# Another split of the scan steps over the engines, and the gate product moved by half a tile

## The reference

```python
def step(h, inp):
    u_t, dt_t, B_t, C_t = inp
    dA = jnp.exp(jnp.clip(dt_t[..., None] * A, -20.0, 0.0))
    dB_u = jnp.clip(dt_t[..., None] * B_t[:, None, :] * u_t[..., None], -10.0, 10.0)
    h = jnp.clip(h * dA + dB_u, -100.0, 100.0)
    y = jnp.einsum('bds,bs->bd', h, C_t)
    return (h, y)
...
y = y * jax.nn.silu(z)
```

## Time and profile before

| | |
|---|---|
| Time, median of 3 runs | 5121.12 us (5117.18 to 5122.27) |
| The profiled execution, its own time | 5121.12 us |
| Its span on the core | 5119.3 us |
| POOL line 2237 (X), 512 instructions | 1190.1 us busy, 2362 ns each |
| POOL line 2244 (Z), 128 instructions | 302.1 us busy, 2360 ns each |
| DVE line 2422 (Z), 256 instructions | 313.5 us busy, 1225 ns each |
| The last copy of `yp` | starts at 4159.86 us |

### The profile page before, as it was taken

The page is one execution under the profiler, slowest core; times in us unless marked ns, Lnnn a source line. Parts: engine busy times, 40 slices in busy tenths (PEclk is TensorE's granted clock), DMA queues, the critical chain, the costliest instruction groups (busy, mean ns, idle before and its releaser), DMA issues. The chain is left out here.

```text
span 5119.3 us, 48377 instructions
## 1 busy us (share of the span) xinstructions
PE 4267.1 (83%) x15605; PEld 2378.9 (46%) x15605; DVE 3493.2 (68%) x3850; ACT 2150.4 (42%) x3741; POOL 2645.8 (52%) x1523
## 2 busy tenths in 40 slices
PE   8997977699999099888748888888888869978886
PEld 6776865344444044333224444444444434435553
DVE  5554347422476456378869999999999967745776
ACT  1111114222354711067736655656655643423442
POOL 4445964000132011057859999999999953312221
PEclk9998986699999599899869999999999989989998
DMA  3422232323487845334451151151151135530000
GB/s 106 117 83 63 80 107 99 133 93 107 158 297 258 342 181 197 133 133 169 171 198 57 59 182 58 57 182 61 55 184 62 51 116 189 197 109 9 34 33 33
DMA packets 364678, 634.08 MB, mean 124 GB/s; under 512 B 67494, under 2 KB 153287, under 8 KB 352274
## 3 DMA queue, kind: packets, MB, share of 16 engines
q1 hardware_dynamic: 327378, 588.07, 32.9%
q10 hardware_dynamic: 37056, 43.00, 2.3%
HBM read 402.83 MB, written 228.15 MB: 123 GB/s over the span
## 5 line engine op out<-in xcount | busy, mean ns | idle before, releaser
L2237 POOL TENSOR_TENSOR sc_X<-sc_Bm,sc_w 128x1024 f32<-128x1024 f32 x512 | 1190.1, 2362 | 25.2 <-DMA sc_Bm<-d_xd 24.9
L2364 PE MATMUL sc_yp<-sc_Z,sc_idn 128*128 128x512 f32 x1536 | 724.6, 605 | 79.7 <-DVE sc_Z L2422 76.7
L2259 ACT ACTIVATE sc_A<-sc_dt,keep_A 128x1024 f32<-128x1024 f32 x512 | 574.7, 1123 | 288.0 <-DVE sc_Z L2422 222.8
L1329 PE MATMUL ff_ps<-ffn_R 128*128 128x512 f32 x1536 | 660.6, 593 | 0.7 <-issue 0.7
L2364 PEld LDWEIGHTS sc_yp<-sc_Z,sc_idn 128*128 128x128 f32 x1536 | 278.2, 192 | 421.7 <-issue 269.7
L1329 PEld LDWEIGHTS ff_ps<-ffn_R 128*128 128x128 f32 x1536 | 291.7, 190 | 364.1 <-issue 363.6
L2351 PE MATMUL sc_yp<-sc_idn,sc_hT 128*128 128x128 f32 x2048 | 262.7, 282 | 131.1 <-ACT sc_hT L2292 131.1
L2244 POOL TENSOR_TENSOR sc_Z<-sc_H,sc_Cm 128x1024 f32<-128x1024 f32 x128 | 302.1, 2360 | 63.1 <-DVE sc_H L2417 63.0
L2351 PEld LDWEIGHTS sc_yp<-sc_idn,sc_hT 128*128 128x128 f32 x2048 | 238.2, 192 | 199.3 <-ACT sc_hT L2292 199.3
L2422 DVE TENSOR_TENSOR sc_Z<-sc_A,sc_Cm 128x1024 f32<-128x1024 f32 x256 | 313.5, 1225 | 8.8
L2292 ACT ACTIVATE sc_hT<-sc_tp,sc_ct 128x128 f32<-128x128 f32 x1024 | 288.8, 366 | 52.2 <-PE sc_tp L2344 52.1
(11 more groups left out here) (380 smaller groups left out, 8124.5 us busy)
## 6 DMA issues: line engine op xcount, KB each, us to landing
sc_Bm<-d_xd SPq DMA_DIRECT2D x64, 512.0 KB, 7.1
ffn_gate_d<-ff_o SPq DMA_DIRECT2D x96, 256.0 KB, 2.2
ffn_up_d<-ff_o SPq DMA_DIRECT2D x96, 256.0 KB, 6.2
ffn_g_d<-ff_z SPq DMA_DIRECT2D x24, 1024.0 KB, 6.5
ffn_R<-ffn_g_d SPq DMA_DIRECT2D x8, 3072.0 KB, 10.9
ffn_R<-ffn_up_d SPq DMA_DIRECT2D x8, 3072.0 KB, 21.3
sc_Cm<-d_xd SPq DMA_DIRECT2D x48, 512.0 KB, 7.5
ffn_R<-ffn_up_d SPq DMA_DIRECT2D x23, 1024.0 KB, 12.9
```

Source lines behind the costliest of these rows:

```text
L1329: last = nc.tensor.matmul(ps[:, 2 + t % 6], w[:, k, h * P:(h + 1) * P], xt[:, n, k], start=(k == 0), stop=(k == KD - 1))
L2237: nc.gpsimd.tensor_tensor(X[:, k % RX], Bm[:, n], w[:, j % 2], ALU.mult).then_inc(db, 1)
L2259: nc.scalar.activation(A[:, k % 2], dt[:, j % 2], ACT.Exp, scale=keepA[:, n:n + 1]).then_inc(ex, 1)
L2364: last = nc.tensor.matmul(yp[:, e * TB:(e + 1) * TB], idn[:], Z[:, zed(k) % RZ, e * TB:(e + 1) * TB], start=(n == 0), stop=(n == NS - 1))
```

## The change

- `ON_POOL` goes from states 3, 6, 9, 12 to 3, 6, 10, 13, and `ON_PE` from 1, 4, 7, 10 to 1, 4, 8, 12. So DVE multiplies for states 0, 2, 5, 7, 9, 11, 14, 15, and no longer for 0, 2, 5, 8, 11, 13, 14, 15. The counts stay 4, 4 and 8.
- PE's gate products move from the first four steps of each 8 to the last four. With that `keep_z` of tile t moves from step 4 of tile t to step 1 of tile t + 1, and the z store from step 7 of tile t to step 3 of tile t + 1. The last `keep_z` and the last z store come after the loops.
- The first loads of the gate's operands come one state later in SP's list.

```diff
--- before.py
+++ after.py
@@ -2050,8 +2050,8 @@
 TC = 1024
 
 
-ON_POOL = (3, 6, 9, 12)
-ON_PE = (1, 4, 7, 10)
+ON_POOL = (3, 6, 10, 13)
+ON_PE = (1, 4, 8, 12)
 
 
 def scan_stage(nc, keepA, flag, ident, win_t, dt_d, w_d, xd_d, xt_d, y_d, z_d):
@@ -2191,9 +2191,9 @@
             load_rows(0)
             for n in range(NS):
                 load_b_c(0, n)
-                if n < KD:
-                    load_xz(0, n)
-                    load_wz(0, n)
+                if 1 <= n <= KD:
+                    load_xz(0, n - 1)
+                    load_wz(0, n - 1)
             load_dt_w(1)
             for k in range(NU_):
                 i, c, n = place(k)
@@ -2220,9 +2220,11 @@
                     load_wz(t + 1, q)
                     if (t + 1) % CB == 0:
                         load_xz(t + 1, q)
-                if k % UZ == UZ - 1:
-                    sp.wait_ge(zev, 1 + t + 1)
-                    sp.dma_start(z_d[t % CB * P:(t % CB + 1) * P, t // CB * TB:(t // CB + 1) * TB], zo[:]).then_inc(zst, 16)
+                if k % UZ == 3 and t:
+                    sp.wait_ge(zev, 1 + t)
+                    sp.dma_start(z_d[(t - 1) % CB * P:((t - 1) % CB + 1) * P, (t - 1) // CB * TB:((t - 1) // CB + 1) * TB], zo[:]).then_inc(zst, 16)
+            sp.wait_ge(zev, 1 + NT)
+            sp.dma_start(z_d[(CB - 1) * P:CB * P, (T // TB - 1) * TB:T], zo[:]).then_inc(zst, 16)
             sp.wait_ge(zst, 1 + NT * 16)
 
         @block.gpsimd
@@ -2314,14 +2316,15 @@
                     decay(k + 2)
                 if n == NS - 1:
                     store(k // NS)
-                if k % UZ == KD:
-                    keep_z(k // UZ)
+                if k >= UZ and k % UZ == 1:
+                    keep_z(k // UZ - 1)
                 if on_pe(n - 1):
                     turn(k - 1, 0)
                 if on_pe(n - 2):
                     turn(k - 2, 1)
                 if n == 0 and c == CB - 1 and i + 1 < NCH:
                     columns(i + 1)
+            keep_z(NT - 1)
             act.wait_ge(yst, 1 + NU_ // NS * 16)
 
         @block.tensor
@@ -2385,8 +2388,8 @@
                     fold(k - 3)
                 if on_pool(n - 2):
                     add(k - 2)
-                if k % UZ < KD:
-                    gate(k // UZ, k % UZ)
+                if k % UZ >= KD:
+                    gate(k // UZ, k % UZ - KD)
                 if on_dve(n):
                     add(k)
```

## The result

The changed kernel takes 5152.44 us (median of 4 runs, 5150.77 to 5156.61), the kernel before 5119.15 us in the same comparison. The ratio is 1.0067, with a 95% interval of 1.0055 to 1.008: slower by 0.67%, by the two medians 33 us. The forecast was 5147 us, in a range of 5124 to 5162. The profiled execution after has a span of 5149.7 us, 30.4 us more than before.

The account below looks back on a forecast made before the run. POOL and DVE, nearly full, wait on each other; the yp copy's chain becomes longest. Steady intervals +24 and +15, round 0 -12.8, boundaries -2, end +2.3 sum to +26.5 on 5121.12: 5147 us, range 5124 to 5162.

Parts of the forecast that it names:

- The chain to the copy of `yp`: After scan of 13: copy at 14.86 us, scan of 2 at 17.70, DVE waits 2.74; rounds 49.1 and 48.85 us.
- The new split: Steady rounds: DVE's run of own products drops from four to three; 1.2 us a round saved if nothing else waited.
- The loop as drawn: POOL and DVE waiting for each other, Z(3) to X(13) and back: rounds of 46.3 and 46.7 us.
- the fast rival: The yp copy stays hidden in steady rounds (path 2.7 us shorter), thirty save 36 us: 5071 us, chance 0.14.
- The moved gate products: On PE: 0.86 us counted in iteration 15; those in 12 to 14 fit into waits, first-half ones hide.
- Round 0: The stage's first round: gate tile 1's first product comes later, next Z(3) 12.8 us earlier; bounds 0 and 16.
- the landing: Arrival of gate tile 1's weights at the start: stays where it was, by DMA ring order, PE waiting until 2653.76.
- PE's wait at the gate: In the first round, before gate tile 1's first product: some 5 us instead of 17.
- The steady rounds' total: 15 intervals without carry at +1.6 us, +24; 15 with carry at +1.0, +15; chunk boundaries -2.
- The boundaries and the end: Three chunk boundaries -2 us, four more steps of lead hiding loads; stage end +2.3: copy 1.8, last stores about 0.5.
- The sum: All terms over the whole kernel: +26.5 us on 5121.12 us, giving 5147.6; chance of this forecast 0.60.

Follow-up runs that it names:

- Experiment 3: The changed kernel with ACT's copy of yp moved behind the decay of step 2 in the next round: 5068.98 us, ratio 0.99.
- experiment 1: The kernel before with only the two new lists of states; gate products, z store and first loads unmoved: 5131.41 us, ratio 1.0023.
- experiment 4: The changed kernel with PE's gate product placed behind the add of the same iteration: 5128.02 us, ratio 1.002.
- experiment 7: The kernel before with the new lists of states and ACT's yp copy behind the next round's decay of step 2: 5075.51 us, ratio 0.9915.
- experiment 2: The kernel before with only gate products, z copy and store and first loads moved, old lists of states: 5144.33 us, ratio 1.0041.
- experiment 9: The changed kernel with PE taking state 11 instead of 12, which DVE multiplies: 5152.24 us, ratio 1.0067.
- Experiment 8: The changed kernel with 16 unused filler matmuls on PE in every round but the first and a chunk's last: 5163.68 us, ratio 1.0092.
- experiment 5: The kernel before with only ACT's yp copy moved behind the next round's decay of step 2: 5115.69 us, ratio 0.9992.
- experiment 6: The kernel before with moved gate products, z store and first loads, and ACT's yp copy behind the next round's decay of step 2: 5103.72 us.

## Why the prediction was right

**The chain to the copy of `yp`.** Shown, and to 0.1 us: the copy 14.78 us behind the scan of 13 (forecast 14.86), the scan of 2 at 17.61 (17.70), DVE's wait 2.59 (2.74), quiet rounds 49.0 and 48.8 us (49.1 and 48.85). Experiment 3 takes only the order in ACT's list away and the wait is gone. Experiments 1 and 4 have one gate product less ahead of the add of 15: experiment 1, where the others are moved back too, gets 0.85 us a round back, and experiment 4 0.73 without carry and 0.5 with it, of the 0.86 us forecast.

**The new split.** The loop as drawn would last 46.3 and 46.7 us, and with the late copy it does (experiments 3 and 7). So the fast rival priced the split rightly. What failed was its condition, a chain 2.7 us shorter, which takes another place for the copy. By occupancy alone POOL was the engine to relieve, as the Trainium skill's page "Perfetto Trace Analysis" has it in its section on the most-contended engine. The trace agrees for the kernel with the late copy, where POOL is busy for 1357.39 of the 1365 us between 2735 and 4100, by its busy times there. In the changed kernel POOL's gap grew: in the same window it is busy for 1281.40 us, before for 1322.63.

**The moved gate products.** In iteration 15 sized right. But I said that those of iterations 12 to 14 fit into PE's waits. That step was wrong. Alone they made the kernel 25 us slower (experiment 2), and experiment 9 shows PE's list nearly continuous there. In the changed kernel both limits coincide: the fold of 12 starts at 2852.93, just as ACT's scaling (2851.76, 1.12 us) and PE's add of 14 (2851.09, 1.88 us) end. That this didn't show in the sum was luck.

**Round 0.** Forecast 12.8 us shorter, measured 12.1. Against SP's first load of the stage (2595.62 before, 2592.04 after) the forecast was met closely. The first product of tile 1 ran 58.1 us behind it before and 58.5 after, so the landing stayed where it was. Z(3) of round 1 was forecast 79.8 us behind it and came 79.3 behind it. The interval is a little longer than forecast because Z(3) of round 0, its other end, lies 1.1 us earlier too, which the forecast didn't have. Two pieces were mis-sized. PE's wait at the gate was 1.58 us and not some 5, since PE was busy with the fold and the adds ahead of it until 2648.95 (3.20 and 4.14 us); this moved nothing, as the landing set the end of the wait. And the product behind it took 1.10 us and not 2.05, which is part of the half microsecond gained.

**The steady rounds' total: mis-sized.** The term "15 intervals at +1.6 and 15 at +1.0, boundaries -2", 37 us, measured 46.7. Thirty intervals at 49.0 and 48.8 would be 1467 us. They took 1479.9. The 13 us of surplus lie in 13 of them, 0.5 to 0.7 us in nine and 1.7 to 2.1 us in four, and they go with the clock. It falls to half 28 times behind round 0, for 3.4 to 10.2 us each, and none of the thirty rounds is free of it, so what tells the long rounds is the place of the fall. Busy times of three falls:

```profile
2717.60:2721.00 3.40, 2.86 (x4) 1.31 (x5) 3.40 (x3) 2.79 (x8) 0.66 (x2) 0.50 0.03 10
...
2772.20:2775.60 3.40, 3.40 (x16) 3.14 (x15) 3.37 (x3) 1.18 (x3) 3.40 (x2) 0.50 0.00 0
...
3209.10:3219.30 10.20, 8.23 (x25) 5.66 (x26) 10.16 (x6) 6.57 (x12) 7.71 (x5) 0.50 0.07 28
```

The first lies on either side of Z(3) at 2720.4, where PE does the add of 2, and costs nothing: both rounds take 49.0 us. The second begins 2.8 us behind a Z(3), in a fold, and its round takes 49.6 us. The third lasts 10.2 us and covers both places, and its round takes 50.8 us. All thirty rounds sort this way. In the 17 short ones the clock is back within 1.9 us of Z(3). In 12 of the 13 long ones it is still at half 5.8 us behind Z(3) or later, and in the last one it falls 24 us behind it. The long round from 3212:

```profile
3215.70 3.77 PE L2354 MATMUL sc_yp<-sc_idn,sc_hT 128*128 128x128 f32 x16 [1.23 <-ACT sc_hT L2294]
...
3227.72 2.36 DVE L2420 TENSOR_TENSOR_SCAN sc_A<-sc_A,sc_hc,sc_X 128x1024 f32<-128x1024 f32 x1 [1.91 <-ACT sc_A L2261]
...
3255.45 1.95 PE L2367 MATMUL sc_yp<-sc_Z,sc_idn 128*128 128x512 f32 x4 [1.19 <-ACT sc_yo L2300]
...
3260.62 3.50 PE L2367 MATMUL sc_yp<-sc_Z,sc_idn 128*128 128x512 f32 x4 [2.78 <-DVE sc_Z L2425]
```

```profile
3212.00:3218.00 6.00, 4.77 (x17) 3.23 (x16) 5.96 (x5) 3.45 (x7) 5.88 (x3) 0.50 0.01 1
```

The fold at 3215.70 takes 3.77 us instead of 2.05, and the granted clock between 3212 and 3218 is 0.50. ACT waits for PE's transposes, and DVE waits 1.91 us for a decay at 3227.72, in the middle of the round. At the end of the round the add at 3260.62 follows 2.78 us of idle PE, and that follows a 1.19 us wait for the copy: this add takes 3.50 us instead of 1.98, and the round behind it still takes 48.8 us. That idle time is new. Before, PE waited 0.6 to 1.5 us at these adds, and its clock stayed at 1.00 there. That the long rounds go with a fall that PE's list can't hide is shown in three kernels (the changed one, experiments 2 and 8). That the new idle time makes the clock fall is argued from its place, and the runs are divided on it. Experiment 1, with the gate products where they were, has 5 falls behind round 0, and experiment 2, with them moved, has 21. But experiment 5, with them where they were and the late copy, has 20. Experiment 8 filled the idle time and the clock did hold there, but fell elsewhere. So why it falls in one round and not in the next stays open.

**The boundaries and the end.** The end gave 1.5 us to the copy (forecast 1.8). What follows the copy took 0.9 us less than before, where the forecast had 0.5 more, and no run looks into that. The loads at the boundaries did what the prediction said. Before, PE waited for one of them at the start of each later chunk, 3.02, 3.54 and 3.48 us, its clock fell to half right there, and DVE lost 0.92 us to a decay at the first of them:

```profile
3020.29 1.13 PE L2373 MATMUL sc_zp<-sc_xz,sc_wz 128*128 128x512 f32 x2 [3.02 <-DMA sc_xz<-d_xt]
...
3027.48 2.35 DVE L2417 TENSOR_TENSOR_SCAN sc_H<-sc_A,sc_hc,sc_X 128x1024 f32<-128x1024 f32 x1 [0.92 <-ACT sc_A L2259]
```

In the changed kernel PE waits for none of these loads. What that is worth can't be read there: the interval at the first boundary took 49.48 us, but the rounds beside it vary by more than the 0.65 us in question. The lead is not the only remedy either. In experiment 5, with the loads as before, PE waits for them in shorter pieces (1.20 and 1.30 us at this place), and the surplus is gone.

**The sum.** Thirty rounds cost 9.7 us more than forecast and round 0 gained 0.7 less. Against that stand Z(3) of round 0, 1.1 us earlier, and an end that cost 0.5 us and not 2.3. The total is 34 us where the forecast had 26.5.

## What to carry to other kernels

When work is spread more evenly over the busiest engines, look at what the last item of a round releases, and at what stands behind the release in its engine's list. Here a copy of one microsecond, in the list of an engine that is 60% busy, decided between 1% faster and 0.7% slower. Cost such a chain piece by piece along each engine that feeds it, since the second branch was only 0.2 us shorter (experiment 9), and shortening one alone brought nothing that could be measured.

## What the runs showed of the hardware that was not expected

TensorE's granted clock fell to half 28 times, for 3.4 to 10.2 us each, in thirty rounds of a loop that keeps PE over 80% busy. In the kernel before it fell 3 times there, each time at one of PE's waits for a load at a chunk's start. In the changed kernel a fall cost 0.5 to 2.1 us where PE's work released the round (a fold of 3.77 instead of 2.05 us). It cost nothing where it met the add of 2 (rounds of 49.0 us on both sides of the fall at 2717.6). In experiment 6, where the late copy had taken PE's list out of the chain, it cost nothing: rounds with a fall 42 us behind Z(3) and rounds with one 3 us behind it last 47.9 us like the others (47.86 us at 0.96 in the one shown). Sixteen added matmuls where PE had stood idle held the clock there, at 1.00, and it fell 25 us later, to 0.76 over 7 us. Less than half the time at the half clock was left, 51 us instead of 123, and the kernel took 11 us more.
